# Dot-product graph attention: a unit's probabilities turned in front of the product of the unit before, with two buffers for the turned probabilities

## The chip, the core and the metric

The kernel runs on one core of a Trainium2 chip. The metric is device time in microseconds (us) of one launch. TensorE (PE) multiplies and writes to PSUM, VectorE (DVE) and ScalarE (ACT) read PSUM and SBUF, GpSimd (POOL) works on SBUF, SyncE (SP) issues the DMAs. Each engine runs its own queue in order; they wait for each other by semaphores.

## The reference, cut to what matters

Four graph attention layers follow each other, each with a residual: `x = x + layer(relu(layernorm(x)))`, for 8 graphs of 1024 nodes with 64 features. The first two are attention by dot products and are the ones that the change touches:

```
# layer 0, one head
scores = einsum('bnd,bmd->bnm', Q, K) / 8
scores = where(adj == 0, -1e9, scores)
out    = softmax(scores, -1) @ V
# layer 1, four heads
scores = leaky_relu(einsum('bhno,bhmo->bhnm', q, k) / 8, 0.2) - 1e10 * (1 - adj)
out    = leaky_relu(mean over heads of softmax(scores, -1) @ v, 0.2)
```

Layers 2 and 3 (additive attention and graph attention with a second norm) follow and are left as they are.

## The kernel before, in words

`dot_layer` is called twice, with `heads` 1 and 4 (`leaky` means four heads). A *unit* is one block of 128 rows of one graph and one head: 8 units per graph in the first layer, 32 in the second, so 64 and 256 units. `n` counts the units in a graph and `u` those of the layer. Six graphs run in a loop (three rounds of two graphs), the last two are written out with fixed addresses.

For every unit the engines do this, each in its own `graph` function:

- PE: `turn_probs` turns the 128 x 1024 probabilities by eight transposes into the PSUM tile `turned` (two banks); `turn_out` multiplies the turned output of the unit before by the value weights into `unit_out`; `score` computes the scores of a later unit in four matmuls (two halves of 512 columns, each of a high and a low part); `fill` projects the next graph, a piece in some units (two pieces turn y by sixteen matmul records, the others take two); `probs_times_values` is the product, 64 x 128 into `outT`.
- ACT: `copy_half` copies the second half of `turned` into `probs_t` in SBUF; `exponentials` takes the softmax's exponentials and their row sums; with four heads, `relu` takes the positive part of the scores; `high_part` takes the high part of a fill.
- POOL: with four heads `mask_relu` adds the mask to the relu, in two adds (`l_masked`); with one head `mask` turns the adjacency into a mask; besides, parts of the next layer norm.
- DVE: `copy_half` copies the first half of `turned`; `finish` scales the unit's output and adds it to `acc` (four heads) or `x_res` (one head), and behind a block's last head takes the leaky relu (`l_leaked`) and the residual; `logit` adds scores and mask and finds the row maximum (the custom operation of line 268); `inverse_sum` takes a reciprocal; `copy_out` copies `outT` into `turned_out`; besides, the fills' low parts, layer norm sums and the values (`take_values`).

What sets the order is the code's order on each queue. Scores have two PSUM buffers, logits, probabilities, relu and masked two SBUF buffers; `turned`, `probs_t` and `outT` one each. Before the change, in iteration u PE runs turn_probs(u), turn_out(u-1), score(u+3), a fill, and the product of u, which waits for `unit_done` of u-1 (DVE's `finish`) and for both copies of u. DVE runs copy_half(u), finish(u-1), logit(u+2), inverse_sum, copy_out(u) and then the extras. ACT runs copy_half(u), exponentials(u+1), relu(u+3).

The four waits on which a unit hangs, word for word:

```
turn_probs:          pe.wait_ge(sems["probs_ready"], u + 1)
                     wait(pe, sems["half0_copied"], STARTS + u)
turn_out:            pe.wait_ge(sems["out_copied"], STARTS + u + 1)
finish:              v.wait_ge(sems["out_turned"], u + 1)
score:               wait(pe, sems["logits_ready"], STARTS + u - 1)
```

Of the kernel before, what the change touches and what calls it, by code (L numbers as in the profile page):

```python
# [31 lines left out]
F32 = mybir.dt.float32  # L32
# [273 lines left out]
def dot_layer(nc, s, layer, heads, w_dram, b_dram, A, adj_dram=None, x_dram=None):  # L306
# [15 lines left out]
    with ExitStack() as ctx:  # L322
# [36 lines left out]
        masked = sb("masked", [P, 2, N], F32) if leaky else None  # L359
        acc = sb("acc", [P, D], F32)  # L360
# [82 lines left out]
        def _(g):  # L443
# [64 lines left out]
            def graph(b, par, last_graph):  # L508


                for n in range(U):
# [14 lines left out]
                    if leaky and not (last_graph and n + 3 >= U):  # L526
                        i = ((n + 3) // H) % NB
                        mask_relu((b + (n + 3) // U) * (NB // 2) + i // 2, i % 2, n + 3, b * U + n + 3)
# [3 lines left out]
            if leaky:  # L532
                for u in range(3):
                    mask_relu(0, 0, u, u)
# [17 lines left out]
        def _(pe):  # L552
# [24 lines left out]
            def score(b, par, n, u):  # L577
# [3 lines left out]
                if n < 3:  # L581
                    pe.wait_ge(sems["fill_copied"], b * K + K)
                    if leaky:
                        pe.wait_ge(sems["staged"], (b + 1) * 16 * (1 + 2 * H))
                rows = slice(i * P, (i + 1) * P)
                for half in range(2):
# [3 lines left out]
                    nc.tensor.matmul(out, h1[:, par, rows], kl[:, par, h, cols], start=False, stop=True).then_inc(sems["scores_ready"], 1)  # L590

# [10 lines left out]
            def graph(b, par, project, last_graph, weights_next=False):  # L602
                for n in range(U):
                    u = b * U + n
                    turn_probs(pe, s, sems, probs[:, n % 2, :], u)
                    if n > 0:
                        turn_out(pe, s, sems, u - 1, 0, unit_out, weights=wv[:, (n - 1) % H, :])
                    if n + 3 < U:
                        score(b, par, n + 3, u + 3)
                    elif not last_graph:  # L610
                        score(b + 1, 1 - par, n + 3 - U, u + 3)
# [10 lines left out]
                    probs_times_values(pe, s, sems, values[:, par, :, :], u)  # L622
# [28 lines left out]
            for u in range(3):  # L651
                score(0, 0, u, u)
            with pe.Fori(0, B // 2 - 1) as t:
                for par in range(2):
                    graph(2 * t + par, par, True, False)
# [4 lines left out]
        def _(a):  # L660
# [14 lines left out]

            def relu(n, u):
# [6 lines left out]
            def graph(b, par, project, last_graph):  # L683
                for n in range(U):
                    u = b * U + n
                    copy_half(a, nc.scalar.copy, s, sems, 1, u)
                    if not (last_graph and n + 1 == U):
                        exponentials(a, s, sems, logits[:, (n + 1) % 2, :], probs[:, (n + 1) % 2, :],
                                     (n + 1) % 4, u + 1)
                    if leaky and not (last_graph and n + 3 >= U):  # L690
                        relu(n + 3, u + 3)
# [9 lines left out]
            if leaky:  # L701
                relu(2, 2)
            with a.Fori(0, B // 2 - 1) as t:
# [6 lines left out]
        def _(v):  # L710
# [61 lines left out]
            def finish(b, n, u):  # L772
# [15 lines left out]
                if h == H - 1:  # L788
                    v.drain()
# [3 lines left out]

            def next_tables(n):

                if n % 2 and n // 2 < A.K:
                    A.take_first(v, n // 2)
# [10 lines left out]
            def graph(b, par, project, last_graph, weights_next=False):  # L808
                for n in range(U):
                    u = b * U + n  # L810
                    v.drain()
                    copy_half(v, nc.vector.tensor_copy, s, sems, 0, u)
                    if n > 0:
                        finish(b, n - 1, u - 1)
                    if not last_graph or n + 2 < U:
                        logit(b, (n + 2) % U, u + 2)
                    inverse_sum(n)
# [4 lines left out]
                    if leaky and n in (0, 2):  # L822
                        mean_half(next_norm(s, b), b + 2, n // 2)
                    if leaky and n in (12, 14):
                        scale_half(b + 2, n // 14)
                    copy_out(v, s, sems, u)
                    for k in fills_at(n, project):
                        take_fill(b + 1, 1 - par, k)
# [6 lines left out]
                    if n == (22 if leaky else 4) and project:  # L835
                        take_values(b + 1, 1 - par)
                v.drain()
                finish(b, U - 1, b * U + U - 1)

# [80 lines left out]
            logit(0, 1, 1)  # L920
            if adj_dram is not None:
# [987 lines left out]
```

## Time and profile before

| what | us |
|---|---|
| median of 3 runs (3452.84 to 3463.19) | 3458.22 |
| the profiled execution, its own time | 3459.63 |
| its span | 3457.8 |
| PE busy in the span | 3048.0 (88%) |
| DVE busy | 3036.1 (88%) |
| ACT busy | 2893.4 (84%) |
| POOL busy | 993.0 (29%) |
| first layer, first to last logits | 25.3 to 246.4 |
| second layer, first to last logits | 296.3 to 1247.8 |

The span is from the first to the last instruction of one execution. The busy shares are means over four layers with different limits: the third layer alone runs from about 1257 to 3120 us, so what concerns the dot layers is read from stretches between 25 and 1257 us. PE's busy time is modelled, since matmuls are pipelined: a row of eight turns that says 1.09 us may be followed by the next matmul after 0.93.

### The profile page before, as it was taken

What the parts mean: (1) busy time and instruction counts of PE and PEld (TensorE: products, weight loads), DVE (VectorE), ACT (ScalarE), POOL (GpSimd) and SP (SyncE); (2) the same over time, 40 slices, a digit from 0 to 9 for tenths busy, and PEclk for the clock granted to TensorE, in tenths of its full rate; (3) what the DMA queues carried; (4) which work ended last, traced back from release to release, by engine and by line L of the source; (5) the groups of instructions that cost most, each with busy time, mean ns of one, the idle gap of its engine ahead of it and who ended that gap; (6) DMA issues with size and microseconds to landing.
All of it is one profiled execution on the core that took longest, in us unless ns stands there. A gap on an engine that the chain in (4) does not pass through costs nothing. (4 is left out here: it accounts for less than half of the span.)

```text
span 3457.8 us, 78785 instructions
## 1 busy us (share of the span) xinstructions
PE 3048.0 (88%) x30972; PEld 1677.1 (49%) x30972; DVE 3036.1 (88%) x4698; ACT 2893.4 (84%) x3774; POOL 993.0 (29%) x869
## 2 busy tenths in 40 slices
PE   7997998989999979999898898998988998877875
PEld 5764666666666643333333333333333333336664
DVE  7886887878888889999999999999999999975676
ACT  4555787777778779999999999999999999975675
POOL 5434666666666610000000000000000000006684
PEclk9998999999999999999999999999999999997798
DMA  7640000000000000000000000000000000002121
GB/s 246 220 146 21 22 22 21 20 21 22 22 20 21 20 10 11 11 11 11 10 11 11 11 11 10 10 11 11 11 10 11 11 11 11 11 4 70 55 63 34
DMA packets 68411, 111.58 MB, mean 32 GB/s; under 512 B 26452, under 2 KB 26582, under 8 KB 68054
## 3 DMA queue, kind: packets, MB, share of 16 engines
q1 hardware_dynamic: 68054, 106.69, 10.0%
q8 instruction: 240, 3.93, 0.5%
q14 instruction: 117, 0.96, 0.1%
HBM read 86.61 MB, written 18.87 MB: 31 GB/s over the span
## 5 line engine op out<-in xcount | busy, mean ns | idle before, releaser
L1308 ACT ACTIVATE l_scalar_ring<-l_w,l_r 128x1024 f32<-128x1024 f32 x1568 | 1651.4, 1154 | 3.9 <-PEq L322 3.5
L1348 DVE TENSOR_SCALAR l_vector_ring<-l_w_code,l_r_code 128x2048 f32<-128x2048 f32 x1264 | 1602.6, 1340 | 3.1 <-PE scores L1240 0.6
L1230 PE MATMUL scores<-l_scalar_ring,l_signs 128*32 128x512 f32 x6272 | 753.0, 598 | 78.4 <-ACT l_scalar_ring L1308 78.1
L1240 PE MATMUL scores<-l_vector_ring,l_signs_code 128*32 128x512 f16 x10112 | 681.8, 393 | 103.7 <-DVE l_vector_ring L1348 102.0
L463 POOL TENSOR_TENSOR l_masked<-l_relu,mask 128x512 f32<-128x512 f32 x512 | 586.1, 1166 | 366.5 <-ACT l_relu L680 345.3
L250 ACT COPY probs_t<-turned 128x512 f32<-128x512 f32 x576 | 324.0, 587 | 420.7 <-PE turned L209 420.7
L172 POOL TENSOR_TENSOR stat<-stat,minus_half 128x8 f32<-128x8 f32 x32 | 71.6, 2238 | 1842.3 <-DVE stat L167 1842.2
L1240 PEld LDWEIGHTS scores<-l_vector_ring,l_signs_code 128*32 128x32 bf16 x10112 | 251.3, 95 | 563.7 <-DVE l_vector_ring L1348 228.9
L277 ACT ACTIVATE l_probs<-l_logits,negmax 128x1024 f32<-128x1024 f32 x384 | 442.8, 1153 | 7.0 <-DVE negmax L268 7.0
L209 PE MATMUL turned<-ident,l_probs 128*128 128x128 f32 x3072 | 436.6, 287 | 11.8 <-issue 7.2
L1230 PEld LDWEIGHTS scores<-l_scalar_ring,l_signs 128*32 128x32 f32 x6272 | 186.5, 109 | 428.1 <-issue 243.8
L220 PE MATMUL outT<-probs_t,l_values 128*64 128x128 f32 x5120 | 352.4, 280 | 40.5 <-DVE l_acc L786 28.1
L209 PEld LDWEIGHTS turned<-ident,l_probs 128*128 128x128 f32 x3072 | 344.3, 145 | 70.8 <-issue 54.1
L268 DVE CUSTOM_DVE_ANT_0 l_logits<-scores,l_masked,l_bound 128x1024 f32<-128x1024 f32 x256 | 327.9, 1281 | 54.7 <-POOL l_masked L463 39.1
L220 PEld LDWEIGHTS outT<-probs_t,l_values 128*64 128x64 f32 x5120 | 277.7, 137 | 171.8 <-DVE l_acc L786 102.9
L250 DVE COPY probs_t<-turned 128x512 f32<-128x512 f32 x320 | 221.2, 691 | 83.7 <-PE turned L209 61.3
L680 ACT ACTIVATE l_relu<-scores 128x512 f32<-128x512 f32 x512 | 275.0, 591 | 4.2 <-PE scores L590 4.1
L589 PE MATMUL scores<-l_kh,l_h 128*128 128x512 f16 x640 | 247.0, 386 | 8.2 <-DMA l_kl<-l_dl 3.3
L590 PE MATMUL scores<-l_kl,l_h 128*128 128x512 f16 x640 | 246.7, 385 | 0.0
L1548 POOL TENSOR_TENSOR l_base<-l_dst_slope,mask 128x512 f32<-128x512 f32 x128 | 153.2, 1224 | 101.1 <-DVE l_dst_slope L1720 90.2
L242 PE MATMUL outT<-l_wv,turned_out 128*128 128x64 f32 x640 | 118.0, 266 | 37.1 <-DVE turned_out L257 36.0
L231 PEld LDWEIGHTS outT<-l_values,probs_t 128*128 128x128 f32 x1024 | 120.7, 194 | 54.4 <-issue 52.8
(243 smaller groups left out, 2840.5 us busy)
## 6 DMA issues: line engine op xcount, KB each, us to landing
mask<-masks_kept SPq DMA_DIRECT2D x192, 256.0 KB, 2.6
l_adj<-adj SPq DMA_DIRECT2D x64, 512.0 KB, 5.8
masks_kept<-l_mask_ring SPq DMA_DIRECT2D x64, 256.0 KB, 5.0
x_res<-x SPq DMA_DIRECT2D x8, 256.0 KB, 5.1
out<-x_res SPq DMA_DIRECT2D x8, 256.0 KB, 2.9
l_h<-l_h SPq DMA_DIRECT2D x8, 128.0 KB, 2.7
l_kl<-l_dh SPq DMA_DIRECT2D x32, 2.0 KB, 1.7
l_kl<-l_dl SPq DMA_DIRECT2D x32, 2.0 KB, 1.7
```

The costliest lines, as they stand in the source:

```text
L209: last = s.nc.tensor.transpose(s.turned[:, j, :], probs[:, j * P:(j + 1) * P], s.ident[:])
L220: last = s.nc.tensor.matmul(s.outT[half * s.D:(half + 1) * s.D, 0:P], values[:, j, :], s.probs_t[:, j, :], start=(j < 2), stop=(j >= s.NB ...
L250: copy(s.probs_t[:, half * n:(half + 1) * n, :], s.turned[:, half * n:(half + 1) * n, :]).then_inc(sems[f"half{half}_copied"], 1)
L268: s.nc.vector.tensor_tensor_reduce(out=out, in0=logits, in1=mask, scale=minus_scale, scalar=3e38, op0=ALU.add, op1=ALU.min, accum_out=s.ne ...
L277: s.nc.scalar.activation(probs, logits, ACT.Exp, bias=s.negmax[:, slot:slot + 1], scale=-1.0, accum_out=total).then_inc(sems["probs_ready" ...
L463: last = nc.gpsimd.tensor_tensor(masked[:, n % 2, cols], relu4[:, n % 2, cols], s.mask[:, i, cols], ALU.add)
L589: nc.tensor.matmul(out, h2[:, par, rows], kh[:, par, h, cols], start=True, stop=False)
L680: nc.scalar.activation(relu4[:, n % 2, half * BANK:(half + 1) * BANK], s.scores[:, n % 2, half, :], ACT.Relu, scale=1.0 / SLOPE - 1.0).the ...
L1230: last = nc.tensor.matmul(s.scores[g * ROWS:(g + 1) * ROWS, buf, half, :], signs[:, window], scalar_ring[:, at % SCALAR_RING, g, halves[ha ...
L1240: last = nc.tensor.matmul(s.scores[g * ROWS:(g + 1) * ROWS, buf, half, :], signs_code[:, par, g % 2, window], parts(vector_ring[:, at % VE ...
L1308: last = nc.scalar.activation(scalar_ring[:, at % SCALAR_RING, g, :], w[:, par, :], ACT.Relu, bias=r[:, par, column:column + 1])
L1348: last = nc.vector.tensor_scalar(vector_ring[:, at % VECTOR_RING, g:g + 2, :], w_code[:, par, :, :], r_code[:, par, 0, column:column + 1], ...
```

## The change

In the dot layers the turn of the probabilities moves one unit ahead of the product: in iteration u PE turns the probabilities of u+1 and then multiplies those of u, which were turned an iteration before. For that `probs_t` gets a second buffer in SBUF; the PSUM tile `turned` stays single. The exponentials move to two units ahead, scores, relu and mask to four, logits to three. On DVE the copy of `turned` moves to the end of the iteration and `copy_out`, the fills and the extras to its front, for the unit before; the leaky relu of a block leaves `finish` for a function of its own, `leak`, which runs an iteration later. Ahead of the loop stand one unit more of scores, relu, mask, exponentials and logits, and the turn and copies of unit 0.

```diff
+        probs_t = [s.probs_t, sb("probs_t", [P, NB, P], F32)]
...
+            def product(par, n, u):
+
+                pe.wait_ge(sems["half0_copied"], STARTS + u + 1)
+                pe.wait_ge(sems["half1_copied"], STARTS + u + 1)
+                wait(pe, sems["out_copied"], STARTS + u)
+                for j in range(NB):
+                    half = j % 2
+                    last = nc.tensor.matmul(s.outT[half * D:(half + 1) * D, 0:P], values[:, par, j, :], probs_t[n % 2][:, j, :],
+                                            start=(j < 2), stop=(j >= NB - 2))
+                last.then_inc(sems["out_ready"], 1)
...
             def graph(b, par, project, last_graph, weights_next=False):
                 for n in range(U):
                     u = b * U + n
-                    turn_probs(pe, s, sems, probs[:, n % 2, :], u)
+                    if not (last_graph and n + 1 == U):
+                        turn_probs(pe, s, sems, probs[:, (n + 1) % 2, :], u + 1)
                     if n > 0:
                         turn_out(pe, s, sems, u - 1, 0, unit_out, weights=wv[:, (n - 1) % H, :])
-                    if n + 3 < U:
-                        score(b, par, n + 3, u + 3)
+                    if n + 4 < U:
+                        score(b, par, n + 4, u + 4)
...
-                    probs_times_values(pe, s, sems, values[:, par, :, :], u)
+                    product(par, n, u)
...
             def graph(b, par, project, last_graph):
                 for n in range(U):
                     u = b * U + n
-                    copy_half(a, nc.scalar.copy, s, sems, 1, u)
+                    if not (last_graph and n + 2 >= U):
+                        exponentials(a, s, sems, logits[:, n % 2, :], probs[:, n % 2, :], (n + 2) % 4, u + 2)
                     if not (last_graph and n + 1 == U):
-                        exponentials(a, s, sems, logits[:, (n + 1) % 2, :], probs[:, (n + 1) % 2, :],
-                                     (n + 1) % 4, u + 1)
-                    if leaky and not (last_graph and n + 3 >= U):
-                        relu(n + 3, u + 3)
+                        copy_turned(n + 1, u + 1)
+                    if leaky and not (last_graph and n + 4 >= U):
+                        relu(n + 4, u + 4)
...
+            def copy_turned(n, u):
+
+                v.wait_ge(sems["turned_ready"], STARTS + u + 1)
+                nc.vector.tensor_copy(probs_t[n % 2][:, 0:NB // 2, :], s.turned[:, 0:NB // 2, :]).then_inc(sems["half0_copied"], 1)
...
                     v.drain()
-                    copy_half(v, nc.vector.tensor_copy, s, sems, 0, u)
                     if n > 0:
-                        finish(b, n - 1, u - 1)
-                    if not last_graph or n + 2 < U:
-                        logit(b, (n + 2) % U, u + 2)
-                    inverse_sum(n)
+                        copy_out(v, s, sems, u - 1)
+                    for k in fills_at(n - 1, project and n > 0):
+                        take_fill(b + 1, 1 - par, k)
...
+                    if n > 1:
+                        leak(b, n - 2)
...
+                    if n > 0:
+                        finish(b, n - 1, u - 1)
+                    if not last_graph or n + 3 < U:
+                        logit(b, (n + 3) % U, u + 3)
+                    inverse_sum(n)
+                    if not (last_graph and n + 1 == U):
+                        copy_turned(n + 1, u + 1)
```

On DVE, in the second layer's loop, a unit without extras as the queue stood before (`l_acc` is `finish`, `l_logits` and `negmax` are the two rows of `logit`, `turned_out` is `copy_out`):

```order
L250 COPY probs_t<-turned 128x512
L786 SCALAR_TENSOR_TENSOR l_acc<-outT,rinv,l_acc 128x64
L739 REGISTER_ALU
L268 ISA l_logits,negmax<-scores,l_masked,l_bound 128x1024
L268 ISA negmax 128x1
L770 RECIPROCAL rinv<-rowsum 128x1
L257 COPY turned_out<-outT 128x128
L250 COPY probs_t<-turned 128x512
```

Here the copy of `turned` opens the round and the copy of `outT` closes it. On DVE at the same place after the change:

```order
L257 COPY turned_out<-outT 128x128
L809 SCALAR_TENSOR_TENSOR l_acc<-outT,rinv,l_acc 128x64
L762 REGISTER_ALU
L268 ISA l_logits,negmax<-scores,l_masked,l_bound 128x1024
L268 ISA negmax 128x1
L793 RECIPROCAL rinv<-rowsum 128x1
L823 COPY probs_t<-turned 128x512
L257 COPY turned_out<-outT 128x128
```

The copy of `turned` has moved to the end of the round, and the copy of `outT`, now of the unit before, to its front.

On PE, in the second layer's loop, a unit without a fill before, with what each first instruction waits for (`turned` is the turn, `outT<-l_wv` turn_out, `outT<-probs_t` the product):

```order
L209 MATMUL turned<-ident,l_probs 128x128 [waits l1_half1_copied,l1_half0_copied,l1_probs_ready]
L209 MATMUL turned<-ident,l_probs 128x128 x7
L242 MATMUL outT<-l_wv,turned_out 128x64 [waits l1_unit_done,l1_out_copied]
L58 REGISTER_ALU
L589 MATMUL scores<-l_kh,l_h 128x512 [waits l1_logits_ready]
L590 MATMUL scores<-l_kl,l_h 128x512
L589 MATMUL scores<-l_kh,l_h 128x512
L590 MATMUL scores<-l_kl,l_h 128x512
L220 MATMUL outT<-probs_t,l_values 64x128 [waits l1_half1_copied,l1_out_copied,l1_half0_copied,l1_unit_done]
L220 MATMUL outT<-probs_t,l_values 64x128 x7
```

The product at the end is of the same unit as the turn at the front. On PE at the same place after the change:

```order
L209 MATMUL turned<-ident,l_probs 128x128 [waits l1_half1_copied,l1_half0_copied,l1_probs_ready]
L209 MATMUL turned<-ident,l_probs 128x128 x7
L242 MATMUL outT<-l_wv,turned_out 128x64 [waits l1_unit_done,l1_out_copied]
L58 REGISTER_ALU
L590 MATMUL scores<-l_kh,l_h 128x512 [waits l1_logits_ready]
L591 MATMUL scores<-l_kl,l_h 128x512
L590 MATMUL scores<-l_kh,l_h 128x512
L591 MATMUL scores<-l_kl,l_h 128x512
L600 MATMUL outT<-probs_t,l_values 64x128 [waits l1_half1_copied,l1_out_copied,l1_half0_copied,l1_unit_done]
L600 MATMUL outT<-probs_t,l_values 64x128 x7
```

PE's rows read alike; what moved is the unit that each belongs to. Before, turn and product of one iteration are of the same unit u. After, the turn is of u+1 and its wait for the two copies is for those of u; the product is of u, whose copies were awaited by the turn already; the scores are those of u+4 instead of u+3.

## Rows read from the trace of the kernel before

**Rows 1.** Busy time by stretch: stretch, length, then PE, PEld, DVE, ACT, POOL busy.

```profile
540.00:660.00 120.00, 112.19 (x1043) 78.45 (x1042) 97.14 (x234) 95.29 (x178) 80.40 (x73) 1.00 0.07 20
```

**Rows 2.** Waits in the four-head layer, 310 to 1240 us: total, times, longest.

```profile
PEld outT L220 <- DVE l_acc L786: 100.4, 155, 4.3
PEld outT L242 <- DVE turned_out L257: 52.7, 87, 1.5
...
DVE l_logits L268 <- POOL l_masked L463: 32.6, 66, 0.8
```

**Rows 3.** Timeline of one undisturbed unit, one-head layer: start, length, engine, line, operation.

```profile
235.17 1.09 PE L209 MATMUL turned<-ident,l_probs 128*128 128x128 f32 x8
...
236.10 0.33 PE L242 MATMUL outT<-l_wv,turned_out 128*128 128x64 f32 x2
...
236.30 0.69 DVE L250 COPY probs_t<-turned 128x512 f32<-128x512 f32 x1 [0.72 <-PE turned L209]
...
236.91 0.27 DVE L779 SCALAR_TENSOR_TENSOR x_res<-outT,rinv,x_res 128x64 f32<-128x64 f32 x1
...
237.10 1.27 DVE L268 CUSTOM_DVE_ANT_0 l_logits<-scores,l_mask_ring,l_bound 128x1024 f32<-128x1024 f32 x1
237.24 0.85 PEld L220 LDWEIGHTS outT<-probs_t,l_values 128*64 128x64 f32 x16 [0.43 <-DVE x_res L779]
...
238.27 1.09 PE L209 MATMUL turned<-ident,l_probs 128*128 128x128 f32 x8
...
238.38 0.29 DVE L257 COPY turned_out<-outT 128x128 f32<-128x128 f32 x1
```

**Rows 4.** Timeline at a graph's end, four-head layer, 409 to 424 us.

```profile
410.99 1.28 DVE L268 CUSTOM_DVE_ANT_0 l_logits<-scores,l_masked,l_bound 128x1024 f32<-128x1024 f32 x1 [0.40 <-POOL l_masked L463]
...
415.09 2.27 POOL L463 TENSOR_TENSOR l_masked<-l_relu,mask 128x512 f32<-128x512 f32 x2 [0.82 <-ACT l_relu L680]
...
416.06 0.43 PE L242 MATMUL outT<-l_wv,turned_out 128*128 128x64 f32 x2 [1.14 <-DVE turned_out L257]
...
416.54 0.28 DVE L786 SCALAR_TENSOR_TENSOR l_acc<-outT,rinv,l_acc 128x64 f32<-128x64 f32 x1 [0.53 <-PE outT L242]
416.92 0.52 DVE L790 SCALAR_TENSOR_TENSOR l_leaked<-l_acc 128x64 f32<-128x64 f32 x1
```

**Rows 5.** Timeline of PE alone, one-head layer, over units with fills.

```profile
114.93 0.43 PE L242 MATMUL outT<-l_wv,turned_out 128*128 128x64 f32 x2 [0.39 <-DVE turned_out L257]
...
118.94 1.09 PE L209 MATMUL turned<-ident,l_probs 128*128 128x128 f32 x8
...
122.89 1.09 PE L209 MATMUL turned<-ident,l_probs 128*128 128x128 f32 x8
...
126.41 1.09 PE L209 MATMUL turned<-ident,l_probs 128*128 128x128 f32 x8
```

**Rows 6.** Timeline of DVE alone over the same stretch.

```profile
115.51 0.28 DVE L779 SCALAR_TENSOR_TENSOR x_res<-outT,rinv,x_res 128x64 f32 x1 [0.64 <-PE outT L242]
...
118.17 0.67 DVE L144 TENSOR_REDUCE stat<-x_res 128x8 f32 x1
...
136.24 0.67 DVE L179 TENSOR_REDUCE stat<-square 128x8 f32<-128x512 f32 x1
```

**Rows 7.** Single lines: ns min/median/max, first and last start in us.

```profile
L268 DVE CUSTOM_DVE_ANT_0 l_logits<-scores,l_masked,l_bound x256: 1273/1283/1286, 296.3 to 1247.8; 128x1024 f32<-128x1024 f32 x128
L268 DVE CUSTOM_DVE_ANT_0 l_logits<-scores,l_mask_ring,l_bound x64: 1273/1276/1285, 25.3 to 246.4; 128x1024 f32<-128x1024 f32 x64
...
L790 DVE SCALAR_TENSOR_TENSOR l_leaked<-l_acc x64: 225/226/523, 317.6 to 1256.5; 128x64 f32<-128x64 f32 x64
...
L732 DVE SCALAR_TENSOR_TENSOR l_values<-y x16: 671/810/1565, 24.5 to 1094.2; 128x512 f32<-128x512 f32 x16
```

**Rows 8.** Timeline, four-head layer, a graph's first logits and a jump back.

```profile
527.32 1.28 DVE L268 CUSTOM_DVE_ANT_0 l_logits<-scores,l_masked,l_bound 128x1024 f32<-128x1024 f32 x1
...
536.61 1.94 PE L209 MATMUL turned<-ident,l_probs 128*128 128x128 f32 x8 [3.44 <-issue]
```

More of the change, by code:

```diff
@@ L532, in _ @@
             if leaky:
-                for u in range(3):
+                for u in range(4):
                     mask_relu(0, 0, u, u)
@@ L580, in score @@
                 wait(pe, sems["logits_ready"], STARTS + u - 1)
[L581 removed]
+                if n < 4:
                     pe.wait_ge(sems["fill_copied"], b * K + K)
@@ L650, in _ @@
             wait(pe, sems["fill_copied"], K)
-            for u in range(3):
+            for u in range(4):
                 score(0, 0, u, u)
+            turn_probs(pe, s, sems, probs[:, 0, :], 0)
             with pe.Fori(0, B // 2 - 1) as t:
@@ L674, in high_part @@
                 last.then_inc(sems["high_ready"], 1)
+            def copy_turned(n, u):
+                a.wait_ge(sems["turned_ready"], STARTS + u + 1)
+                nc.scalar.copy(probs_t[n % 2][:, NB // 2:NB, :], s.turned[:, NB // 2:NB, :]).then_inc(sems["half1_copied"], 1)
             def relu(n, u):
@@ L702, in _ @@
                 relu(2, 2)
+            exponentials(a, s, sems, logits[:, 1, :], probs[:, 1, :], 1, 1)
+            if leaky:
+                relu(3, 3)
+            copy_turned(0, 0)
             with a.Fori(0, B // 2 - 1) as t:
@@ L787, in finish, with leak @@
                                                    in1=acc[:], op0=ALU.mult, op1=ALU.add).then_inc(sems["unit_done"], 1)
-                if h == H - 1:
-                    v.drain()
+            def leak(b, n):
+                if leaky and n % H == H - 1:
+                    xb = s.block(b, n // H)
                     nc.vector.scalar_tensor_tensor(out=leaked[:], in0=acc[:], scalar=SLOPE, in1=acc[:], op0=ALU.mult, op1=ALU.max)
@@ L821, in graph @@
                         layer_norm_scale(v, s, sems, next_norm(s, b), b + 2)
-                    if leaky and n in (0, 2):
+                    if leaky and n in (1, 3):
                         mean_half(next_norm(s, b), b + 2, n // 2)
[L824 to L828, printed above, removed]
+                    if leaky and n in (13, 15):
+                        scale_half(b + 2, n // 15)
+                    if n > 1:
+                        leak(b, n - 2)
                     if weights_next and n == 24:
@@ L834, in graph @@
                         next_tables(n)
-                    if n == (22 if leaky else 4) and project:
+                    if n == (23 if leaky else 5) and project:
                         take_values(b + 1, 1 - par)
+                    if n > 0:
[5 more added lines that the diff above has]
+                        copy_turned(n + 1, u + 1)
                 v.drain()
+                copy_out(v, s, sems, b * U + U - 1)
                 finish(b, U - 1, b * U + U - 1)
+                if leaky:
+                    v.drain()
+                    leak(b, U - 1)
             nc.vector.memset(one[:], 1.0)
@@ L920, in _ @@
             logit(0, 1, 1)
+            logit(0, 2, 2)
+            copy_turned(0, 0)
             if adj_dram is not None:
```

13 lines of the change are left out of this document (7 added, 6 removed).

## The prediction

> **What bounds the kernel now.** I read three views in order. First the busy time by stretch: in the middle of the four-head layer TensorE (PE) is busy 112 of 120 us, VectorE (DVE) 97, ScalarE (ACT) 95, GpSimd (POOL) 80 [rows 1]. Nothing is full by a wide margin, so the question is which chain of waits closes a unit. Then the waits of that layer: PE's weight loads for the product wait 100.4 us for DVE's `l_acc` (the step that adds the unit before), those for the output turn 52.7 us for DVE's `turned_out`, and DVE's logits wait 32.6 us for POOL's masked scores [rows 2]. Then one undisturbed unit of the one-head layer in order of time [rows 3]. With T for the eight turns of the probabilities, TO for the output turn, P for the product: T starts at 235.17, TO at 236.10, P at 237.24, the next T at 238.27. A unit costs PE 3.10 us there; P waits for DVE's add, but only so far that PE loses little. DVE has finished its round before the next T ends: its copy of the turned probabilities waits 0.72 us for PE. So before, **PE sets the pace** in a plain unit, and whatever DVE or PE do besides (fills, layer norm, leak, values) comes partly on top: the mean is (246.4 - 25.3)/63 = 3.51 us per unit in the one-head layer and (1247.8 - 296.3)/255 = 3.73 in the four-head layer [rows 7]; of the latter a graph of 32 units without the jump back takes 527.32 - 410.99 = 116.3 [rows 4, 8].
>
> The profiled execution has a span of 3457.8 and a time of 3459.6, against a median of 3458.2; I sum against 3459.6. Only the two dot layers are touched, 64 and 256 units.
>
> **The change: what is on the path.** No arithmetic is added. In the loop PE issues T for unit u+1 ahead of TO(u-1), the scores of u+4 and P(u); before, P(u) used the T of its own iteration. So P no longer waits for a copy, and the product's buffer in SBUF is doubled. What isn't doubled is the PSUM tile `turned`: T(u+2) may start only when both halves of `turned` for u+1 are copied. DVE's half of this copy has moved from the front of its round to the very end, behind `finish` and the logits. And `finish(u-1)` needs TO(u-1), which PE runs behind T(u+1). This closes a ring with no slack in it:
>
> T(u+1) -> TO(u-1) -> finish(u-1) -> logits(u+3) -> copy(u+1) -> T(u+2).
>
> Each step has a row. T to TO: 0.93 [rows 3]. TO to finish where DVE waited: 416.06 to 416.54 = 0.48, that is 0.05 behind a TO of 0.43 that stood alone [rows 4]; right behind T a TO takes 0.33 [rows 3], so I take 0.37. Finish to logits: 236.91 to 237.10 = 0.19. Logits to the DVE operation behind its reciprocal: 237.10 to 238.38 = 1.28. The copy: 0.69. From the copy's end to PE's first load 0.07, as between the add's end and P's load (236.91 + 0.27 to 237.24, 0.06) [rows 3]. Sum: 0.93 + 0.37 + 0.19 + 1.28 + 0.69 + 0.07 = **3.53 us**, against PE's 3.10 now. The bounds: 0.10 lower or higher would need a TO that ends otherwise (0.37 to 0.48) or waits of the logits that show once DVE has really stood still (the row shows 0.19 where it hadn't). I keep 3.53, the sum of the nearest rows, and 3.65 as the upper end. In the looped graphs of the one-head layer, finish came 0.58 behind a TO (114.93 to 115.51) instead of 0.48 [rows 5, 6]; I add 0.11 for those 48 units: 3.64.
>
> **What hides now.** In the ring DVE stands from the copy's end to finish for 0.07 + 0.93 + 0.37 = 1.37 us. Into this gap the change has put copy_out, the fills' low parts, layer norm's sums, the leak and the values. Copy_out and the drain ahead of it take about 0.3, so 1.07 is free. A fill's part (about 0.7) fits and costs nothing; before it did cost. PE has 3.53 - 3.10 to spare: a fill of two matmuls makes PE's unit 126.41 - 122.89 = 3.52, just covered; a fill that turns y makes it 122.89 - 118.94 = 3.95, 0.42 too much [rows 5]. The queues that lie off the ring: exponentials two units ahead are issued right behind the logits and end before T's turn; scores four ahead keep their distance to the logits, but ACT now issues the relu in front of the exponential of the next unit, so POOL starts earlier and the 32.6 us [rows 2] go. SP's mask loads are triggered by POOL as before, one unit sooner. All of these have slack of some tenths and are costed at nothing; if POOL's cover went, the old 32.6 us would be the price.
>
> **Four-head layer, per graph of 32.** 32 x 3.53 = 113.0. Two y fills: 2 x 0.42 = 0.8. The values, up to 1.56 in this layer [rows 7], exceed the gap once: 0.6. The graph's end, where TO follows P directly and the leak stands on the ring: 0.2. Variance and small overlaps: 0.4. The leak of every fourth unit: 0.7 in the clear, hidden; but it reads two SBUF tensors, and where a POOL add is running it waits: `l_leaked` takes 0.52 at 416.92 beside the add that runs from 415.09 to 417.36, and 0.225 otherwise [rows 4, 7]. POOL's adds take 2.27 of each 3.53, and by the order above the second is running when the leak comes, until some 1.2 behind T's start; that would push finish by 0.35. Ends 0 and 0.35, I take half: 8 x 0.17 = 1.4. Sum 116.4 against 116.3: **no change**, and the rest of the layer (two jumps back of the loop, 3.44 of PE's idle time in one [rows 8]; the next layer's tables) is kept as it is. The Trainium skill's page "SBUF — State Buffer", section "SBUF: two separate sides", says that DVE operations with two SBUF inputs and GpSimd's share a port pair as an exclusive lock for the whole instruction. The trace agrees with 0.52 against 0.225; by that rule alone every leak would pay, 64 x 0.35 = 22 us instead of 11.
>
> **One-head layer, per graph of 8.** 8 x 3.64 = 29.1; the first unit, whose layer norm mean (0.67 and more [rows 6]) now stands on the ring and whose y fill is on PE, +0.7; the second y fill, 3.95 - 3.64 = +0.3; variance (0.67 [rows 6]) and values (0.67 at least [rows 7]) both in one gap, +0.4: 30.5, against 8 x 3.51 = 28.1. Eight graphs: +19, less about 2 for the two graphs with fixed addresses (3.53): **+17**.
>
> **Ends.** Ahead of each loop, T(0) now stands behind the scores of unit 3 and DVE's first copy behind the logits of unit 2; at the end one round is nearly empty. I estimate +2.5 per layer from these rows' durations (one logits and one scores step of about 1.3 and 0.9 more to fill the pipe): **+5**.
>
> Sum: 0 + 17 + 5 = +22, 3459.6 + 22 = **3482 us**.
>
> **Rivals.**
> *A longer ring.* If DVE, once it has really waited for TO, needs longer to get through the waits of the logits, or PE through the three waits of T, 3.53 becomes 3.65: 320 x 0.12 = +38, 3520. For it: rows show these steps only where the engine was not standing. Against: P's load follows the add by 0.06 with several waits in front.
> *The gap hides everything.* No leak meets POOL (-11), fixed and looped graphs alike (-5): 3466, no measurable difference (0.3%, about 10 us, is what a measurement of this kernel can tell).
> *Faster: PE stays the bound.* The 100.4 and 52.7 us of PE's waits go [rows 2] and nothing takes their place; place: the start of T. It decides if the ring is shorter than PE's own unit: 32 x 3.10 + 10 x 0.42 + 2 x 0.85 = 105 per graph, 11 less than now, 8 x 11 + about 5 in the one-head layer = -93: 3367. Against it is the order itself: the copy stands behind the logits, 1.28 + 0.69 behind finish, and T behind the copy. The Trainium skill's page "Perfetto Trace Analysis", section "Matmuls" (under "Optimizing Tensor Performance"), wants independent matmul groups to rotate through PSUM banks so that one's evacuation overlaps the next group; here `turned` has one set, so by that rule this gain needs a second set, which the change doesn't make. No run here shows it yet.
> *The change does not turn ahead.* T could be held back as far as P was, and PE's wait only moves from P to T. That is what the ring says; its time is the forecast's.
>
> **How the numbers follow.** Forecast (3470 to 3500) 0.52; longer ring (3500 to 3540) 0.20; everything hidden (3455 to 3470) 0.20; faster 0.08. Leaving out the last and the tip of the second: 3458 to 3525. Slower by over 0.3%: 0.72; within: 0.20; faster: 0.08.
>
> **What the profile after would show.** T to T 3.53 in plain units; PE waiting at T for DVE's `probs_t` copy by about 0.4 in most units, some 130 us in all, and no longer at P; DVE idle ahead of finish until TO, up to 1 us; DVE's copy of `turned` no longer waiting for PE; the one-head layer longer, the four-head layer about equal. Wrong would be: T that doesn't wait for the copy, a T to T near 3.1, or leaks that stretch to 1 us and push finish in every fourth unit.

## The result: 1.1% slower, and the profile after

The kernel after takes 3496.9 us in the median of 4 runs (3491.4 to 3501.3), the one before 3455.9 (3452.8 to 3463.2): a ratio of 1.0112, interval 1.0091 to 1.0133. The forecast was 3482 in a range of 3458 to 3525. The profiled execution has a span of 3496.4, 38.6 more than before. First the single line of the logits after, whose first and last starts cut the span into stages (ns min/median/max, first and last start in us), to be held against [rows 7]:

```profile
L268 DVE CUSTOM_DVE_ANT_0 l_logits<-scores,l_masked,l_bound x256: 1267/1283/1286, 321.2 to 1274.9; 128x1024 f32<-128x1024 f32 x128
L268 DVE CUSTOM_DVE_ANT_0 l_logits<-scores,l_mask_ring,l_bound x64: 1272/1283/1286, 25.5 to 269.8; 128x1024 f32<-128x1024 f32 x64
...
L268 DVE CUSTOM_DVE_ANT_0 l_logits<-scores,l_base x64: 1221/1225/1226, 3161.0 to 3468.9; 128x1024 f32<-128x1024 f32 x64
```

The one-head layer grew from 221.1 to 244.3 us (+23.2), the four-head layer from 951.5 to 953.7 (+2.2). Start and the gaps behind the two layers grew by 4.0 in all. That is +29.4 from the start to the third layer's first logits, where the code that the change touches lies. The fourth layer, whose code is the same, took 307.9 instead of 298.0 (+9.9); the rest is -0.7.

One undisturbed unit of the four-head layer after, DVE and PE in order of time (start, length, engine, line, operation, idle time before and what ended it):

```profile
663.98 1.06 PE L209 MATMUL turned<-ident,l_probs 128*128 128x128 f32 x8 [0.60 <-issue]
...
664.88 0.33 PE L242 MATMUL outT<-l_wv,turned_out 128*128 128x64 f32 x2
...
665.26 0.28 DVE L809 SCALAR_TENSOR_TENSOR l_acc<-outT,rinv,l_acc 128x64 f32<-128x64 f32 x1 [0.99 <-PE outT L242]
...
665.51 1.28 DVE L268 CUSTOM_DVE_ANT_0 l_logits<-scores,l_masked,l_bound 128x1024 f32<-128x1024 f32 x1
...
666.79 0.67 DVE L823 COPY l_probs_t<-turned 128x512 f32<-128x512 f32 x1
...
667.56 1.06 PE L209 MATMUL turned<-ident,l_probs 128*128 128x128 f32 x8 [0.46 <-issue]
```

This is the ring of the prediction, link by link: 0.90, 0.38, 0.25, 1.28 and 0.77 make 3.58, against 3.53 foreseen. Before, in the plain unit of [rows 3], DVE's copy waited 0.72 for PE; now it starts right behind the logits, and PE stands 0.46 ahead of its next turn. The profile puts that wait down to "issue" and names no releaser; that it is the copy is shown by the experiments, not by this row.

The same in a looped unit of the one-head layer:

```profile
175.87 1.06 PE L209 MATMUL turned<-ident,l_probs 128*128 128x128 f32 x8 [0.26 <-issue]
...
176.77 0.33 PE L242 MATMUL outT<-l_wv,turned_out 128*128 128x64 f32 x2
...
177.25 0.29 DVE L802 SCALAR_TENSOR_TENSOR x_res<-outT,rinv,x_res 128x64 f32 x1 [0.44 <-PE outT L242]
...
177.63 1.28 DVE L268 CUSTOM_DVE_ANT_0 l_logits<-scores,l_mask_ring,l_bound 128x1024 f32<-128x1024 f32 x1
...
178.91 0.67 DVE L823 COPY l_probs_t<-turned 128x512 f32<-128x512 f32 x1
...
179.68 1.06 PE L209 MATMUL turned<-ident,l_probs 128*128 128x128 f32 x8 [0.69 <-issue]
```

0.90, 0.48, 0.38, 1.28, 0.77: 3.81, against 3.64 foreseen. In the last graphs of the layer, which are written out with fixed addresses, the same unit takes 3.60 (turns at 257.49 and 261.09), with these links:

```profile
258.39 0.33 PE L242 MATMUL outT<-l_wv,turned_out 128*128 128x64 f32 x2
258.76 0.28 DVE L802 SCALAR_TENSOR_TENSOR x_res<-outT,rinv,x_res 128x64 f32<-128x64 f32 x1 [0.99 <-PE outT L242]
259.04 1.28 DVE L268 CUSTOM_DVE_ANT_0 l_logits<-scores,l_mask_ring,l_bound 128x1024 f32<-128x1024 f32 x1
```

Output turn to finish is 0.37 here and finish to logits 0.28: the loop adds 0.11 to the one and 0.10 to the other. What stands there in the loop and not in the fixed graphs is register work on DVE's queue, for the address that finish writes (line 802) and for the values that the logits wait for (lines 765 and 766); these are its rows (ns min/median/max, first and last start):

```profile
L802 DVEq FUSED_REGOPS  x48: 57/57/57, 38.5 to 223.7; - x48
```

```profile
L765 DVEq FUSED_REGOPS  x48: 53/53/64, 34.5 to 220.4; - x48
```

```profile
L766 DVEq ALU_OP  x48: 40/40/52, 34.6 to 220.5; - x48
```

48 times, once in each looped unit: 0.053 + 0.040 is nearly all of the 0.10 between finish and logits; 0.057 is half of the 0.11 ahead of finish, and the other half stays unexplained. The four-head loop has one such operation between finish and logits (line 762, 0.040 us, 192 times): the step takes 0.25 there and 0.20 in the layer's last graph, which has fixed addresses.

The waits of the four-head layer after, 310 to 1240 us (total, times, longest), in place of [rows 2]:

```profile
PEld turned L209 <- issue: 136.5, 240, 3.7
DVE l_acc L809 <- PE outT L242: 89.5, 166, 1.0
...
PEld outT L600 <- DVE l_acc L809: 56.1, 129, 1.3
```

PE's wait ahead of the turn and DVE's ahead of finish are the two standing places of the ring. The wait of the logits for POOL, 32.6 us before, is down to 7.0.

### The profile page after: what moved, and what is told of

Read it like the earlier page. It is cut to its first block and busy times, and to the rows that moved or that the text cites. A ratio compares the mean times of both kernels' runs of the same rounds, so it can differ in the third digit from the quotient of the medians.

```text
span 3496.4 us, 78766 instructions
## 1 busy us (share of the span) xinstructions
PE 3034.5 (87%) x30972; PEld 1675.9 (48%) x30972; DVE 3058.6 (87%) x4698; ACT 2942.8 (84%) x3774; POOL 990.2 (28%) x869
## 5 line engine op out<-in xcount | busy, mean ns | idle before, releaser
L209 PE MATMUL turned<-ident,l_probs 128*128 128x128 f32 x3072 | 429.4, 285 | 121.8 <-issue 113.9
L250 ACT COPY probs_t<-turned 128x512 f32<-128x512 f32 x256 | 137.2, 592 | 117.6 <-PE turned L209 117.5
L600 PE MATMUL outT<-probs_t,l_values 128*64 128x128 f32 x2560 | 175.9, 280 | 4.4 <-DVE l_acc L809 3.6
L600 PE MATMUL outT<-l_probs_t,l_values 128*64 128x128 f32 x2560 | 175.1, 278 | 2.1 <-DVE l_acc L806 1.0
L693 ACT COPY probs_t<-turned 128x512 f32<-128x512 f32 x160 | 93.8, 586 | 92.1 <-PE turned L209 92.1
L600 PEld LDWEIGHTS outT<-probs_t,l_values 128*64 128x64 f32 x2560 | 137.9, 137 | 69.3 <-DVE l_acc L809 54.3
L600 PEld LDWEIGHTS outT<-l_probs_t,l_values 128*64 128x64 f32 x2560 | 138.5, 136 | 60.3 <-issue 35.7
```

Of the source, the lines that this page charges most:

```text
L209: last = s.nc.tensor.transpose(s.turned[:, j, :], probs[:, j * P:(j + 1) * P], s.ident[:])
L600: last = nc.tensor.matmul(s.outT[half * D:(half + 1) * D, 0:P], values[:, par, j, :], probs_t[n % 2][:, j, :], start=(j < 2), stop=(j >= N ...
```

## The experiments

Every kernel below is the changed one with the edit shown (`...` stands for lines left out); ratios are to the kernel before, measured beside it.

**DVE's copy moved to the front.**

```diff
+                    if not (last_graph and n + 1 == U):
+                        copy_turned(n + 1, u + 1)
                     if n > 0:
                         finish(b, n - 1, u - 1)
...
                     inverse_sum(n)
-                    if not (last_graph and n + 1 == U):
-                        copy_turned(n + 1, u + 1)
```

> The changed kernel, with one thing moved on VectorE: its copy of the turned probabilities of u+1 stands in front of the add of u-1 and of the logits, instead of behind them. Everything else of the change stays (turn one unit ahead, two buffers, exponentials two ahead, scores four). Ring theory: the next turn then waits only for turn (1.1 us) plus copy (0.7), well under TensorE's own 3.10 us, so turn to turn falls from 3.58 (four heads) and 3.81 (one head) to about 3.1 to 3.3 plus fills; 256 x 0.28 + 64 x 0.35 = about 95 us less than the changed kernel's 3497, so 3400 (3375 to 3440), faster than the kernel before (3456). Rival A (VectorE's own work in the new order is the bound, whatever stands where): about 3490. Rival B (half of it: the add now comes 0.6 us later, the product waits for it and the extras find no room, so that it is back at the kernel before): 3445 to 3465.

Measured: 3414.8 us, ratio 0.9881 (0.9863 to 0.9898). The one-head layer takes 224.8 us, the four-head layer 895.3. A plain unit on DVE:

```profile
623.68 1.27 DVE L268 CUSTOM_DVE_ANT_0 l_logits<-scores,l_masked,l_bound 128x1024 f32<-128x1024 f32 x1
...
625.97 0.69 DVE L823 COPY l_probs_t<-turned 128x512 f32<-128x512 f32 x1 [0.57 <-PE turned L209]
626.57 0.27 DVE L809 SCALAR_TENSOR_TENSOR l_acc<-outT,rinv,l_acc 128x64 f32<-128x64 f32 x1
626.77 1.27 DVE L268 CUSTOM_DVE_ANT_0 l_logits<-scores,l_masked,l_bound 128x1024 f32<-128x1024 f32 x1
```

The unit is 3.09, the copy waits for PE again, and two lines in another place turn a loss of 1.1% into a gain of 1.2%. The copy's place is worth 82 us, 78 of them in the two layers.

**The waits of the logits ahead of finish.** This asks why finish to logits takes 0.38 in the loop.

```diff
+            def logit_waits(u):
 
                 wait(v, sems["probs_ready"], u - 1)
+                if not leaky:
+                    v.wait_ge(sems["scores_ready"], 2 * u + 2)
+                    v.wait_ge(sems["mask_ready"], u + 1)
...
+                    if not last_graph or n + 3 < U:
+                        logit_waits(u + 3)
                     if n > 0:
                         finish(b, n - 1, u - 1)
                     if not last_graph or n + 3 < U:
-                        logit(b, (n + 3) % U, u + 3)
+                        logit(b, (n + 3) % U, u + 3, waited=True)
```

> The changed kernel; in the loop VectorE passes the logits' waits that are long fulfilled (exponentials done, with one head also scores and mask ready) in front of the add instead of between add and logits. No wait is taken away. In the changed kernel the logits start 0.38 us behind the add with one head in the looped graphs and 0.25 with four heads, where the kernel before had 0.19. Theory (the waits are gone through only once the add has been released, so they stand on the ring): one head 0.38 to about 0.20, 48 units x 0.18 = 9 us less, turn to turn 3.81 to 3.63; four heads keep one wait and change by under 0.03 a unit, under 8 us; 3480 to 3490. Rival (the gap is VectorE's own, whatever stands in the queue): 0.38 stays, 3497.

Measured: 3496.4 us, ratio 1.0122 (1.0101 to 1.0144): no gain, and the 3480 to 3490 of the theory was missed. The looped one-head unit fell to 3.70, but a four-head unit rose by up to 0.1; the one-head layer takes 241.9 us, 2.4 less, the four-head layer 962.0, 8.3 more. The one-head links:

```profile
174.82 0.33 PE L242 MATMUL outT<-l_wv,turned_out 128*128 128x64 f32 x2
...
175.37 0.28 DVE L808 SCALAR_TENSOR_TENSOR x_res<-outT,rinv,x_res 128x64 f32 x1 [0.52 <-PE outT L242]
...
175.57 1.27 DVE L268 CUSTOM_DVE_ANT_0 l_logits<-scores,l_mask_ring,l_bound 128x1024 f32<-128x1024 f32 x1
```

Finish to logits is 0.20, so the waits with their register work were what stretched it, but the output turn to finish went from 0.48 to 0.55. Passing them earlier moves a part of their cost to the other side of finish and saves 0.11 a unit, in the looped one-head units alone.

**The leak left out.**

```diff
-                    if n > 1:
-                        leak(b, n - 2)
...
-                if leaky:
-                    v.drain()
-                    leak(b, U - 1)
```

> The changed kernel without the leaky relu of the four-head layer and its residual (two VectorE operations for each of 64 blocks are left out, so that layer adds nothing to x). Theory (a leak that meets a GpSimd add takes about 0.96 us instead of 0.23 and pushes the add by what no longer fits the gap): units with a leak fall from 3.72 to 3.58, 56 x 0.14 = 8 us, and the graph's end, where it stands on the ring, by 0.4 to 0.7, 8 times, 4 us: 12 us less, 3485. Rival 1 (the leak is hidden altogether, 3.72 has another cause): 4 us less, 3493. Rival 2 (the leak costs each time the whole 0.7 by which it is longer): 45 us less, 3452.

Measured: 3472.7 us, ratio 1.0052 (1.0038 to 1.0066). The four-head layer takes 939.1 us, 14.6 less, against 12 expected; a plain looped graph takes 115.6 instead of 118.1. Of the 24 us between the medians the layer explains 15; the profiled fourth layer, whose code is the same, was 13 us shorter too (see the fourth layer below).

**Both moves together** (the first edit and the second).

> Both moves of the two runs above: the copy ahead of the add, and the fulfilled waits ahead of the add. Ring theory: with the copy out of the ring the short waits lie beside TensorE's work, so the time is that of the copy moved alone, within 5 us. Rival (they delay VectorE's round, which is the bound then): about 9 to 15 us less than the copy moved alone.

Measured: 3409.8 us, ratio 0.9874 (0.9856 to 0.9892). The layers take 224.4 and 896.4, within 1.1 us of the copy's move alone: off the ring the waits cost nothing that can be measured.

**The copy kept last, PE's order changed.** If the ring theory holds, another link may be cut and the copy may stay where the change put it.

```diff
-                    if not (last_graph and n + 1 == U):
-                        turn_probs(pe, s, sems, probs[:, (n + 1) % 2, :], u + 1)
-                    if n > 0:
-                        turn_out(pe, s, sems, u - 1, 0, unit_out, weights=wv[:, (n - 1) % H, :])
                     if n + 4 < U:
                         score(b, par, n + 4, u + 4)
...
+                    if n > 0:
+                        turn_out(pe, s, sems, u - 1, 0, unit_out, weights=wv[:, (n - 1) % H, :])
+                    if not (last_graph and n + 1 == U):
+                        turn_probs(pe, s, sems, probs[:, (n + 1) % 2, :], u + 1)
```

> DVE's order is that of the change, the copy of `turned` stays last; only PE's order differs: the scores of u+4 first, then the output turn of u-1, then the turn of u+1, then the product. Ring theory: what costs is that the output turn stands behind a turn which waits for the copy. With the output turn free of it, the ring is copy 0.67, copy_out 0.31, about 0.12 until the output turn, 0.40 to finish, 0.25 to the logits, 1.29 to the next copy = 3.04 us, below PE's own 3.07 to 3.10, and the turn ends 0.8 before DVE wants it. So a plain unit takes about 3.1, a four-head graph 107 to 113 (118 with the change), the program 3400 to 3435. Rival: the copy's place behind the logits costs by itself, whatever PE does in front of it (the product waits for both halves as before): units stay at 3.5 or more and the program at 3480 or more.

Measured: 3502.2 us, ratio 1.0129 (1.0106 to 1.0153): my expectation of 3400 to 3435 missed. The fixed one-head units did fall to 3.14, the looped ones to 3.35, but the four-head units alternate 3.30 and 4.07. A slow one:

```profile
577.44 1.28 DVE L268 CUSTOM_DVE_ANT_0 l_logits<-scores,l_masked,l_bound 128x1024 f32<-128x1024 f32 x1 [0.31 <-POOL l_masked L464]
...
577.72 0.59 ACT L693 COPY l_probs_t<-turned 128x512 f32<-128x512 f32 x1 [0.73 <-PE turned L209]
...
578.20 1.09 ACT L699 ACTIVATE l_relu<-scores 128x512 f32<-128x512 f32 x2
...
578.88 2.27 POOL L464 TENSOR_TENSOR l_masked<-l_relu,mask 128x512 f32<-128x512 f32 x2 [1.64 <-ACT l_relu L699]
```

With the turn later, ACT's copy waits, the relu queues behind it, POOL starts late, and the logits wait for POOL. By this reading a second ring had taken the first one's place, again through an in-order queue; the next experiment tests it.

**And the relu ahead of ACT's copy**, besides.

```diff
-                    if not (last_graph and n + 1 == U):
-                        copy_turned(n + 1, u + 1)
                     if leaky and not (last_graph and n + 4 >= U):
                         relu(n + 4, u + 4)
+                    if not (last_graph and n + 1 == U):
+                        copy_turned(n + 1, u + 1)
```

> e5_scores_first with one more step: on ACT the relu of u+4 goes ahead of the copy of the turned probabilities instead of behind it. Second-ring theory: in e5 the one-head units of the fixed graph did come down to 3.14, as the ring theory said, but the four-head units alternate 3.30 and 4.07, because ACT's copy now waits for a later turn (0.73), the relu and POOL's adds queue behind it, and DVE's logits wait for POOL (0.31). With the relu ahead of the copy POOL starts about 0.6 earlier, the four-head units settle at 3.1 to 3.3, a graph at 107 to 113 (120.9 in e5), and the program at 3410 to 3445; the one-head layer stays as in e5 (238 us). Rival: POOL is not what alternates the units (the scores wait for the logits of two units before, 61 us): then graphs stay within 2 us of 120 and the program at 3490 or more.

Measured: 3403.1 us, ratio 0.9833 (0.9805 to 0.9862), a little below the lower end. The four-head layer takes 871.8 us, the best of all, with the copy last:

```profile
641.36 0.41 PE L242 MATMUL outT<-l_wv,turned_out 128*128 128x64 f32 x2
...
641.60 1.04 PE L209 MATMUL turned<-ident,l_probs 128*128 128x128 f32 x8
641.81 0.28 DVE L809 SCALAR_TENSOR_TENSOR l_acc<-outT,rinv,l_acc 128x64 f32<-128x64 f32 x1 [0.53 <-PE outT L242]
642.06 1.28 DVE L268 CUSTOM_DVE_ANT_0 l_logits<-scores,l_masked,l_bound 128x1024 f32<-128x1024 f32 x1
...
643.34 0.67 DVE L823 COPY l_probs_t<-turned 128x512 f32<-128x512 f32 x1
...
644.72 1.04 PE L209 MATMUL turned<-ident,l_probs 128*128 128x128 f32 x8
```

Finish no longer stands behind the turn; the turn runs beside the logits. Turn to turn is 3.12, and scores cover DVE's copy on PE. The copy behind the logits is harmless as such: what cost was finish behind the output turn behind the turn behind the copy.

**DVE copies half as much.**

```diff
-                nc.vector.tensor_copy(probs_t[n % 2][:, 0:NB // 2, :], s.turned[:, 0:NB // 2, :]).then_inc(sems["half0_copied"], 1)
+                nc.vector.tensor_copy(probs_t[n % 2][:, 0:2, :], s.turned[:, 0:2, :]).then_inc(sems["half0_copied"], 1)
...
+            for t in probs_t:
+                nc.vector.memset(t[:, 2:4, :], 0.0)
```

> The change as it is, but DVE copies only two of its four blocks of the turned probabilities (128x256 instead of 128x512), so two blocks of eight enter the product as zeros; everything else is kept. Ring theory: DVE's copy is a link of the ring with nothing beside it. By the two copies from PSUM in the traces (128x128 0.29, 128x512 0.67) 128x256 takes 0.41, 0.26 less; a four-head plain unit goes from 3.58 to 3.32, a one-head one from 3.81 to 3.55, which is still above PE's 3.1; 256 x 0.26 + 50 x 0.26 = 79 us less, 3418 (3405 to 3440). Rival: the turn is held by PE's own issue (the records name issue, not the copy, ahead of it): no change, 3490 to 3500.

Measured: 3433.6 us, ratio 0.9925 (0.9901 to 0.9950), inside the expected range. Finish to finish, four-head:

```profile
643.51 0.28 DVE L809 SCALAR_TENSOR_TENSOR l_acc<-outT,rinv,l_acc 128x64 f32<-128x64 f32 x1 [0.99 <-PE outT L242]
643.78 1.28 DVE L268 CUSTOM_DVE_ANT_0 l_logits<-scores,l_masked,l_bound 128x1024 f32<-128x1024 f32 x1
...
645.06 0.41 DVE L823 COPY probs_t<-turned 128x256 f32<-128x256 f32 x1
...
646.84 0.28 DVE L809 SCALAR_TENSOR_TENSOR l_acc<-outT,rinv,l_acc 128x64 f32<-128x64 f32 x1 [0.99 <-PE outT L242]
```

0.26 less in the copy is 0.26 less in the unit: 3.32, and 3.55 in the looped one-head layer, both as expected. So it is the copy that PE's "issue" waits for. The layers lost 55.9 us, not 79, mainly since units that hold a leak (3.73) or a long fill (3.95) stayed as long as they were.

**The leak in two pieces**, on top of the copy's move: the leaky relu ahead of the copy, the residual add behind it.

```diff
+            def leak_add(b, n):
+
+                if leaky and n % H == H - 1:
+                    xb = s.block(b, n // H)
                     v.drain()
                     nc.vector.scalar_tensor_tensor(out=xb, in0=leaked[:], scalar=1.0 / H, in1=xb, op0=ALU.mult, op1=ALU.add)
...
+                    if not (last_graph and n + 1 == U):
+                        copy_turned(n + 1, u + 1)
+                    if n > 1:
+                        leak_add(b, n - 2)
                     if n > 0:
                         finish(b, n - 1, u - 1)
```

> e1_copy_first, with the two steps of the leak taken apart: the leaky relu stays ahead of the copy of `turned`, the residual add comes behind it. Contention theory: in e1 the residual add takes 0.93 instead of 0.22 us because it starts inside POOL's add, and the copy, the finish and the product queue behind it, so that a unit with a leak takes 3.67 instead of 3.1. Behind the copy it starts when the add of POOL has ended or is about to: the unit takes about 3.4, 64 x 0.29 = 18 us less than e1, 3397 (3385 to 3408). Rival: the leak costs by its own two steps and drain (0.22 + 0.17 + 0.22) wherever it stands, and taking it apart moves nothing: within 6 us of e1, 3415.

Measured: 3431.9 us, ratio 0.9913 (0.9882 to 0.9944), worse than the copy's move alone; neither theory had that. In 31 units that hold a leak the time between logits went from 3.7 to 4.0 up to 4.96. One of them:

```profile
618.17 2.28 POOL L464 TENSOR_TENSOR l_masked<-l_relu,mask 128x512 f32<-128x512 f32 x2 [0.62 <-ACT l_relu L699]
...
621.30 2.27 POOL L464 TENSOR_TENSOR l_masked<-l_relu,mask 128x512 f32<-128x512 f32 x2 [0.85 <-ACT l_relu L699]
```

```profile
619.33 1.20 DVE L816 SCALAR_TENSOR_TENSOR l_leaked<-l_acc 128x64 f32<-128x64 f32 x1
...
621.32 1.21 DVE L823 SCALAR_TENSOR_TENSOR x_res<-l_leaked,x_res 128x64 f32 x1 [0.19 <-issue]
```

Each row of POOL holds two adds. Here each step of the leak started just behind the start of an add and ended 0.08 us behind its end, 1.2 us for work of 0.22. The contention is right, its dodging was not: in these units the second step met the next add instead of the gap. Where it did miss the adds, it took 0.23, and such a unit as little as 3.42, near the 3.4 expected.

**Each layer in its own best order**: the one-head layer with the copy first, the four-head layer with scores, relu and copy as above.

> The one-head layer in the order of e1_copy_first (turn first on PE, DVE's copy ahead of finish), the four-head layer in the order of e9 (scores first on PE, relu ahead of the copy on ACT, DVE's copy last). If the two layers don't depend on each other, each keeps its own time: first to last logits 225 in the one-head layer (238 in e9) and 872 in the four-head layer (895 in e1), so 13 less than e9: 3390 (3378 to 3402). Rival: the four-head layer's gain in e9 came with the phase in which the one-head layer leaves POOL and the mask loads, and goes again: then its layer is above 880 and the program at 3400 or more.

Measured: 3389.3 us, ratio 0.9812 (0.9777 to 0.9846), faster than both kernels. The layers:

```profile
L268 DVE CUSTOM_DVE_ANT_0 l_logits<-scores,l_masked,l_bound x256: 1270/1283/1287, 306.5 to 1179.6; 128x1024 f32<-128x1024 f32 x128
L268 DVE CUSTOM_DVE_ANT_0 l_logits<-scores,l_mask_ring,l_bound x64: 1272/1275/1284, 25.6 to 254.6; 128x1024 f32<-128x1024 f32 x64
```

229.0 and 873.1: the four-head layer keeps its time, the one-head layer came 4 us longer than expected. These lie in its first graph alone: 32.5 us from its first logits to the next graph's, against 28.5 with the copy's move; the other graphs agree within 0.1. From 29.5 to 41 us TensorE's mean granted clock was 0.55 here, mostly the lower of its two levels (1.2 and 2.4 GHz), and 1.00 there, and eight turns took 1.94 us instead of 1.06. At the start of that stretch PE stood 2.83 us for DVE here and 1.98 there. So the two orders do go together.

## Why the prediction was right, and where its sizes were off

- **The ring** was right: its links are there, and three different cuts (the copy moved, PE and ACT reordered, the copy halved) shorten the unit as it says. The four-head unit is 3.58 for 3.53.
- **Finish to logits** is the term that was mis-sized: 0.19 taken, 0.25 and 0.38 measured. The row it came from shows a DVE that hadn't stood still; the same register work and waits lay in its queue, but show only once DVE waits for the output turn. With fixed addresses the step is 0.20 with four heads and 0.28 with one; the loop adds the register work, 0.04 and 0.09. The prediction had this as the rival of a longer ring (3.65 throughout); it happened in the looped one-head units: 3.81 for 3.64 over 48 units is 8 us. That is more than the whole error of this layer, +23.2 instead of +17.
- **The four-head layer** came at +2.2 for a forecast of 0, but not by graphs that stay equal, and in part by luck. The plain looped graphs rose by 1.8 (116.3 to 118.1, forecast 116.4), the first seven graphs by 7.0 together, and the last one, with the next layer's tables in it, fell from 126.2 to 121.4, which the prediction didn't count. That last graph before and after (length, then PE, PEld, DVE, ACT, POOL busy, granted clock):

```profile
1121.60:1247.80 126.20, 110.74 (x966) 78.40 (x961) 105.58 (x249) 83.67 (x156) 76.12 (x69) 0.96 0.05 14
```

```profile
1153.50:1274.90 121.40, 104.98 (x972) 75.28 (x970) 101.40 (x249) 89.16 (x155) 75.69 (x69) 1.00 0.05 14
```

  Before, PE stood 2.12 and 3.78 us for DVE's `l_acc` there, and the turns that followed took 1.97 us instead of 1.09, at the lower of the two clock levels; after, its longest wait in this graph is 0.84 and the mean granted clock 1.00, as in the other changed kernels (0.99 to 1.00). PE was busy 5.8 us longer before, so the clock can account for these 4.8 us; whether the change raises it there, by shorter waits, was not tested.
- **The leak** was priced right in the mean by a wrong mechanism. I took half of 0.35 for each. Its first step took over 0.4 us in 51 of the 64 blocks, and this line has its times (ns min/median/max):

```profile
L816 DVE SCALAR_TENSOR_TENSOR l_leaked<-l_acc x64: 215/962/1235, 346.9 to 1285.8; 128x64 f32<-128x64 f32 x64
```

  The gap ahead of finish swallows most of that: a unit with a leak takes 3.73, 0.15 more than a plain one. A leak of 1 us that pushes finish in every fourth unit stood in the prediction as a sign of being wrong, and it came: the cost of the leak was about right (14.6 us by the kernel without it, 11 summed), its way was not. In the kernel with scores and relu first, where the leak falls between POOL's adds, the median is 217.
- **Ends**: +4.0 for +5. Two small terms of the sum don't follow from their rows: values of 1.56 exceed a gap of 1.07 by 0.5 and not 0.6, and 0.58 is 0.10 above 0.48 and not 0.11; together that is under 2 us.
- **The profile after** was foreseen in T to T, DVE's idle time, the wait at T and the copy that no longer waits. "No longer at P" was wrong: P still waits 56.1 us for the add, which now comes late; by the ring PE would stand at T otherwise, which no run here separates.
- **The faster rival**, PE as the bound, lost as argued from the order of the queues. The Trainium skill's page "Perfetto Trace Analysis", section "Matmuls", wants independent matmul groups to rotate through PSUM banks, and I took from it that the gain needs a second set of `turned`. The runs show otherwise for this kernel: with one set the plain units come to 3.09 with the copy first and to 3.12 with scores and relu first.
- **The fourth layer's 9.9 us** were in no term. Its stretch before and after (length, then PE, PEld, DVE, ACT, POOL busy, granted clock):

```profile
3132.80:3430.80 298.00, 236.96 (x1968) 197.78 (x1968) 204.76 (x441) 204.16 (x319) 209.54 (x175) 0.86 0.20 58
```

```profile
3161.00:3468.90 307.90, 248.13 (x1968) 206.37 (x1968) 206.10 (x440) 204.12 (x319) 208.69 (x175) 0.83 0.20 56
```

  The same instructions, DVE, ACT and POOL as busy as before, PE busy 11 us longer at a mean granted clock of 0.83 instead of 0.86. In the profiles of all eleven kernels here this layer takes from 291.8 us at 0.90 to 307.9 at 0.83. Whether the change makes the lower clock likelier or it fell so in these runs is open. Without it the sum of the touched code, +29.4, would have been 3489. The other executions point the same way: over the 33 of the kernel before that were measured beside the experiments, the time falls by about 18 us for each 0.01 of mean granted clock (0.962 to 0.973), and at the same clock the four of the kernel after lie 29 to 36 us above that line, where the medians differ by 41.

## What to carry to other kernels

When a step is turned ahead to free one wait, follow the single buffer that is left round all in-order queues: if its copy stands behind work that waits for the next use of the same chain, the buffer closes a ring, and a second buffer elsewhere (here `probs_t`) doesn't open it. Sum that ring link by link from rows in which the engine really stood waiting: in a row of a running engine the waits and the register work in its queue don't show, here 0.06 to 0.19 us at one link. Then look for the cheapest cut: here moving one copy, or letting independent work (the scores) run while the copy is made, and after each cut look for the next ring.

## What the hardware showed besides

- A small DVE step with two SBUF inputs of 128x64, 0.22 us alone, took 1.20 us where it started just behind a POOL add of 1.16. In the ten kernels that have a leak, 473 of its steps took over 0.4 us, and each of them ended 0.08 to 0.09 us behind the end of an operation of POOL, wherever in it the step had started. The Trainium skill's page "SBUF — State Buffer", section "SBUF: two separate sides", calls the port pair an exclusive lock for the whole instruction; these starts and ends agree with it.
- Register work for addresses and wait values, 0.04 to 0.06 us a piece on DVE's queue, shows in no busy time and hides while DVE is ahead. On a ring it counts: a looped one-head unit takes 3.81 and one with fixed addresses 3.60, and 0.15 of these 0.21 us are the three pieces above; the rest is unexplained.
